# Operand transposes moved from TensorE to SP's DMA queue, and masking joined with the row maxima, in a three-stage graph kernel

## The chip, the cores and the metric

The kernel runs on one core of one Trainium2 chip. The metric is the device time of one execution in microseconds (us); the figure quoted is the median of three runs.

## What is computed

128 graphs of 128 nodes with 256 features each pass through one transformer layer (8 heads of 32, an additive bias and a mask from the adjacency matrix, an MLP of width 1024) and then through two single-head graph layers. Cut to what matters:

```python
nx = ln(x, ln1_g, ln1_b);  q, k, v = nx @ wq + bq, nx @ wk + bk, nx @ wv + bv     # 8 heads of 32
bias = where(adj > 0, 0.1 * adj * adj, -inf)
x1 = x + softmax(q @ k.T / sqrt(32) + bias) @ v @ wo + bo
x2 = x1 + gelu(ln(x1, ln2_g, ln2_b) @ w1 + b1) @ w2 + b2
for l in 0, 1:                                   # x starts as x2
    s = where(adj == 0, -1e10, (x @ Wq[l].T + bq[l]) @ (x @ Wk[l].T + bk[l]).T / sqrt(128))
    x = layer_norm(x + where(adj == 0, 0, softmax(s)) @ x @ Wc[l].T)
```

## The kernel before, in words

The graphs are worked in 32 groups of four (`B = 4`), so that one group has 512 rows of 256 features. Weights stay in SBUF. Float32 products are made of three float16 ones (`mm3`, lines 241 to 245): each operand is split into a high half (a cast) and a low half (what the cast lost).

A product needs its operand with the features on the partitions, while normalisations and residuals have the rows there. So five times for each group a block of 128 x 1024 values is turned: `N.xT` (normalised x, for q, k and v), `A.oT` (attention output, for `wo`), `M.mT` (normalised x1, for the MLP), `C0.xT` and `C1.xT` (the operands of the two graph layers). In each, TensorE makes 8 transposes of 128x128 float32 into PSUM (helper `transposes`, line 812, against the identity `ident`), ScalarE casts the result from PSUM into the high half (`xT_h`, `rot_h` or `cT_h`; lines 467, 493, 496, 513), and VectorE subtracts that from PSUM into the low half (`xT_l`, `rot_l`, `cT_l`; lines 654, 695, 710, 725).

For the softmax of the transformer layer, VectorE does two instructions for each graph over its 8 heads: `A.S` (line 673) scales the scores in PSUM, adds `biasA` and writes `area` in SBUF; `A.max` (line 678) reduces to the negated row maxima `nmax`. ScalarE then takes the exponential head by head (line 483). In a graph layer the same is `C.S` (line 731) and `C.max` (line 734), once for the four graphs.

There is no automatic scheduler. Five lists (`TENSOR`, `SCALAR`, `VECTOR`, `GPSIMD`, `SYNC`) give for each engine the order of its steps within one period. An entry such as `M.up3-2` is step `up3` of stage `M`, done for the group that lies two behind; one pass through a list is one period and the passes go over the 32 groups, so that about five groups are in work at once. Each step waits on semaphores for its inputs, and for the last reader of what it overwrites; on an engine everything is strictly in list order. `freed` (before each step of TensorE) holds the waits on PSUM banks.

SP's queue carries all steady DMA traffic: 12 small copies a group that stack q and k on 96 partitions for the scores (`Q.stk`, `qkS`), the load of x, two loads of the adjacency (`adj_in`), and the store of the result.

The steps that the prediction speaks of, on TensorE: `A.AV3` to `A.wo` (attention output of the last graph to the output projection), and `A.wo` to `M.up0` (the projection to the first MLP product). Between the latter lie `x1` (line 701), its statistics (lines 567 and 572), an inverse root on GpSimd (lines 396 and 398), the normalisation (line 580), and the turn `M.mT`.

Of the kernel before, what the change touches and what calls it, by code (L numbers as in the profile page):

```python
# [1073 lines left out]
```

## Time and profile before

| | |
|---|---|
| median of three runs | 2197.3 us (2193.87 to 2198.27) |
| the profiled execution | 2195.11 us, span 2193.1 us |
| busy: TensorE / VectorE / ScalarE / GpSimd | 2016.2 / 1721.4 / 1558.7 / 961.0 us |
| mean granted TensorE clock | 0.971 of full speed |
| DMA | 108.62 MB, mean 50 GB/s |

A busy time is the time in which an engine had at least one instruction in work; matmuls overlap one another, so their count times their mean length is more than it. A row of a group of instructions gives its busy time, the mean length of one in nanoseconds, and the idle time of the engine just before them. Idle time of an engine that is not the bottleneck costs nothing.

### The profile page before, as it was taken

Reading aid. Unit: us, or ns where it says so; the run is one execution under the profiler, and the core shown is the slowest. Engines: PE = TensorE matmul, PEld = TensorE weight load, DVE = VectorE, ACT = ScalarE, POOL = GpSimd, SP = SyncE. Lnnn points to the kernel's source line nnn. Section 1 sums busy time; section 2 is a strip of 40 time slices with the busy share of each in tenths; the row PEclk is TensorE's granted clock in tenths of the full one; section 3 lists DMA queues with packets and bytes.
Section 4 is the critical chain, followed back from the end, with each engine's and each line's share of the span. In section 5 each row is a group of like instructions: output and inputs, shape, how many; then the busy total and the mean of one; then the engine's idle time right before and its main releaser. Section 6 shows DMA issues by size and latency. Waiting matters only on the chain.

```text
span 2193.1 us, 45905 instructions
## 1 busy us (share of the span) xinstructions
PE 2016.2 (92%) x16984; PEld 1499.2 (68%) x16984; DVE 1721.4 (78%) x3397; ACT 1558.7 (71%) x2994; POOL 961.0 (44%) x1304
## 2 busy tenths in 40 slices
PE   5589899999999999999999999999999999999853
PEld 4356677777777777777777777777777777777531
DVE  4566788888888888888888888888888888887422
ACT  2367777777788777777787777777877777777521
POOL 2022344445454454444554544445545444544434
PEclk8799999999999999999999999999999999999976
DMA  3211012222211122222111222222111222210000
GB/s 106 73 49 42 28 45 58 59 59 56 58 49 42 33 59 59 59 59 54 49 42 35 57 58 59 59 54 57 43 39 44 59 59 59 54 50 16 15 10 19
DMA packets 103675, 108.62 MB, mean 50 GB/s; under 512 B 9824, under 2 KB 78432, under 8 KB 103456
## 3 DMA queue, kind: packets, MB, share of 16 engines
q1 hardware_dynamic: 102912, 104.90, 17.9%
q8 instruction: 138, 2.26, 0.4%
q0 software_dynamic: 544, 0.80, 0.2%
q14 instruction: 81, 0.66, 0.1%
HBM read 38.55 MB, written 16.78 MB: 25 GB/s over the span
## 4 chain that ended last, share of the span: by engine, by line
PE 72%; ACT 13%; DVE 6%; POOL 4%; issue 3%; DMA 2%; SPq 1%; DVEq 0%; POOLq 0%; ACTq 0%
PE ps L243 18%; PE ps L245 17%; PE ps L244 17%; PE ps L812 5%; PE ps L972 5%; PE ps L1046 5%; ACT area L483 4%; PE ps L1026 3%; POOL x L403 3%; ACT cs L525 2%; DMA out<-x 2%; ACT area L533 2%; ACT L525 2%; PE ps L965 1%; ACT cq L518 1%
## 5 line engine op out<-in xcount | busy, mean ns | idle before, releaser
L483 ACT ACTIVATE area<-area,nmax 128x128 f32<-128x128 f32 x1024 | 312.5, 390 | 0.8
L243 PE MATMUL ps<-w_h,hid_h 128*128 128x256 f16 x1024 | 279.1, 273 | 6.0 <-POOL hid_l L250 5.1
L245 PE MATMUL ps<-w_h,hid_l 128*128 128x256 f16 x1024 | 279.0, 272 | 0.0
L244 PE MATMUL ps<-w_l,hid_h 128*128 128x256 f16 x1024 | 279.0, 272 | 0.0
L396 POOL TENSOR_TENSOR ve<-mv,eps_cols 128x4 f32<-128x4 f32 x128 | 25.7, 201 | 572.0 <-DVE mv L572 572.0
L250 POOL TENSOR_TENSOR hid_l<-area,hid_h 128x512 f16<-128x512 f32 x128 | 151.8, 1186 | 251.9 <-ACT hid_h L506 251.9
L503 ACT ACTIVATE area<-ps,b_col 128x512 f32<-128x512 f32 x256 | 176.3, 689 | 77.9 <-PE ps L245 76.8
L403 POOL TENSOR_TENSOR x<-xh,cg_row 128x256 f32<-128x256 f32 x128 | 89.0, 728 | 295.7 <-DMA out<-x 272.6
L243 PE MATMUL ps<-rot_h,w_h 128*128 128x512 f16 x512 | 194.4, 380 | 6.2 <-ACT area L503 2.9
L245 PE MATMUL ps<-rot_h,w_l 128*128 128x512 f16 x512 | 194.0, 379 | 0.0
L244 PE MATMUL ps<-rot_l,w_h 128*128 128x512 f16 x512 | 193.9, 379 | 0.0
L518 ACT ACTIVATE ck<-ps,cb_col 128x512 f32<-128x512 f32 x64 | 44.1, 689 | 199.0 <-PE ps L245 199.0
L673 DVE SCALAR_TENSOR_TENSOR area<-ps,biasA 128x1024 f32<-128x1024 f32 x128 | 155.0, 1211 | 37.9 <-PE ps L965 37.9
L403 POOL TENSOR_TENSOR x<-x,cb_row 128x256 f32<-128x256 f32 x256 | 178.2, 728 | 5.0
L506 ACT CAST hid_h<-area 128x512 f16<-128x512 f32 x256 | 158.3, 618 | 8.1
L681 DVE SCALAR_TENSOR_TENSOR pT<-ps,pT 128x1024 f16<-128x1024 f32 x128 | 155.7, 1216 | 3.2 <-ACT pT L489 3.2
L812 PE MATMUL ps<-ident,area 128*128 128x128 f32 x1024 | 135.6, 276 | 21.6 <-DVE area L580 19.0
L678 DVE TENSOR_REDUCE nmax<-area 128x8 f32<-128x1024 f32 x128 | 154.8, 1210 | 0.2
L972 PE MATMUL ps<-ident,area 128*128 128x128 f32 x1024 | 136.3, 276 | 16.4 <-ACT area L483 11.3
L972 PEld LDWEIGHTS ps<-ident,area 128*128 128x128 f32 x1024 | 113.0, 141 | 45.2 <-DVE area L673 22.8
L243 PE MATMUL ps<-cw_h,cT_h 128*128 128x256 f16 x512 | 139.6, 273 | 3.9 <-DVE cs L731 3.9
L245 PE MATMUL ps<-cw_h,cT_l 128*128 128x256 f16 x512 | 139.6, 273 | 0.0
(178 smaller groups left out, 6214.0 us busy)
## 6 DMA issues: line engine op xcount, KB each, us to landing
qkS<-qk SPq DMA_DIRECT2D x384, 128.0 KB, 2.4
xin<-in_x SPq DMA_DIRECT2D x32, 512.0 KB, 3.8
adj_in<-in_adj SPq DMA_DIRECT2D x64, 256.0 KB, 2.9
out<-x SPq DMA_DIRECT2D x32, 512.0 KB, 3.9
area<-in_L_gnn_w SPq DMA_DIRECT2D x2, 1024.0 KB, 11.3
area<-in_L_gnn_Wc SPq DMA_DIRECT2D x2, 256.0 KB, 11.3
area<-in_L_gnn_wq SPq DMA_DIRECT2D x1, 256.0 KB, 3.7
area<-in_L_gnn_wk SPq DMA_DIRECT2D x1, 256.0 KB, 4.0
```

What stands on the lines that cost most here:

```text
L243: pe.matmul(dst, lh, rh, start=start, stop=False, **kw)
L244: pe.matmul(dst, lh, rl, start=False, stop=False, **kw)
L245: return pe.matmul(dst, ll, rh, start=False, stop=stop, **kw)
L403: last = pool.tensor_tensor(dst[:, b], src[:, b], row, op)
L483: last = act.activation(sc[:, b % 2, h], sc[:, b % 2, h], ACT.Exp, bias=nmax[:, b, h:h + 1])
L503: act.activation(hidden[:, b % 2, :], psUp, ACT.Gelu, bias=b1_col[:, b:b + 1], scale=1.0 / W_SCALE).then_inc(a_gelu, 1)
L506: act.copy(hid_h[:, b % RING, :], hidden[:, b % 2, :]).then_inc(a_hi, 1)
L673: dve.scalar_tensor_tensor(sc[:, b % 2], psA_heads, 1.0 / QK_SCALE, biasA[:, b].unsqueeze(1).broadcast_to([P, H, P]), ALU.mult, ALU.add).t ...
L678: dve.tensor_reduce(nmax[:, b, :], sc[:, b % 2], AX.X, ALU.max, negate=True).then_inc(d_max, 1)
L681: dve.scalar_tensor_tensor(pT16[:, b % 2, 1], psA_heads, P_SCALE, pT16[:, b % 2, 0], ALU.mult, ALU.subtract).then_inc(d_PT, 1)
L812: last = pe.transpose(dst[:, c, b * P:(b + 1) * P], rows[:, b, c * P:(c + 1) * P], ident[:, :])
L972: last = pe.transpose(psA_heads[:, h], sc[:, b % 2, h], ident[:, :])
```

## The change

It does two things, and gives all five lists new orders.

1. The transposes on TensorE go. ScalarE now casts the float32 rows themselves, before turning, into a float16 staging tile in SBUF (`sN_h`, `sA_h`, `sC_h`); VectorE subtracts into a second one (`sN_l`, `sA_l`, `sC_l`). SP then issues one DMA transpose for each half, 128x1024 float16 (8 blocks of 128x128), from the staging tile into `xT`, `rot` or `cT`. That is ten DMA transposes for each group. Consumers wait for both (`m_xT`, `m_oT`, `m_mT`, `m_cT`, of `TURN` = 32 for a pair).
2. `A.S` and `A.max` become one `tensor_tensor_reduce` per head, 8 for each graph, and `C.S` and `C.max` one per graph, 4 for each layer. They write negated scores (unscaled sum times -1/QK_SCALE) and their minimum; the exponential has `scale=-1.0`. `biasA`'s factor takes in `QK_SCALE`.

```diff
-SYNC = ["Q.stk-2", "N.ld-1", "Q.ldA-1", "M.ldC-3", "C1.sto-6"]
+SYNC = ["Q.stk-1", "N.ld+0", "M.mT-2", "C0.xT-3", "N.xT+0", "M.ldC-3", "Q.ldA+0", "C1.sto-5",
+        "C1.xT-4", "A.oT-1"]
...
+            def turn(g, dst_h, dst_l, src_h, src_l, a_made, d_made, m_done):
+
+                need_apart(sp, a_made, g, 1, 1)
+                sp.dma_start_transpose(dst_h.rearrange("p c (b t) -> p (c b) t", t=P),
+                                       src_h.rearrange("p c b d -> p (c b d)")).then_inc(m_done, 16)
+                need_apart(sp, d_made, g, 1, 1)
+                sp.dma_start_transpose(dst_l.rearrange("p c (b t) -> p (c b) t", t=P),
+                                       src_l.rearrange("p c b d -> p (c b d)")).then_inc(m_done, 16)
...
+                    elif what == "mT":
+
+                        need_apart(sp, t_wo, g, 1, 1)
+                        turn(g, rot_h, rot_l, sA_h, sA_l, a_mT, d_mT, m_mT)
...
-                        need(act, t_mT, g, 1, 1)
-                        act.copy(rot_h[:, :, :], psM).then_inc(a_mT, 1)
+                        need(act, d_xh[1], g, 1, 1)
+                        need(act, m_oT, g, TURN, TURN)
+                        act.copy(sA_h[:, :, :, :], by_chunk(xhat)).then_inc(a_mT, 1)
...
-                                                  bias=nmax[:, b, h:h + 1])
+                                                  bias=nmax[:, b, h:h + 1], scale=-1.0)
...
-                        dve.tensor_tensor(rot_l[:, :, :], psM, rot_h[:, :, :], ALU.subtract)\
+                        need(dve, m_oT, g, TURN, TURN)
+                        dve.tensor_tensor(sA_l[:, :, :, :], by_chunk(xhat), sA_h[:, :, :, :], ALU.subtract)\
...
-                        dve.scalar_tensor_tensor(sc[:, b % 2], psA_heads, 1.0 / QK_SCALE,
-                                                 biasA[:, b].unsqueeze(1).broadcast_to([P, H, P]),
-                                                 ALU.mult, ALU.add).then_inc(d_S, 1)
-                    elif stage == "A" and what[:3] == "max":
-                        need(dve, d_S, g, B, b + 1)
-                        dve.tensor_reduce(nmax[:, b, :], sc[:, b % 2], AX.X, ALU.max, negate=True).then_inc(d_max, 1)
+                        for h in range(H):
+                            last = dve.tensor_tensor_reduce(sc[:, b % 2, h], psA_heads[:, h], biasA[:, b],
+                                                            scale=-1.0 / QK_SCALE, scalar=HIGHEST,
+                                                            op0=ALU.add, op1=ALU.min,
+                                                            accum_out=nmax[:, b, h:h + 1])
+                        last.then_inc(d_S, 1)
...
-                            dve.tensor_tensor(cs[:, l], psC_S, biasC[:, g[1]], ALU.add).then_inc(d_cS[l], 1)
-                        elif what == "max":
-                            need(dve, d_cS[l], g, 1, 1)
-                            dve.tensor_reduce(cmax[:, l], cs[:, l], AX.X, ALU.max, negate=True).then_inc(d_cmax[l], 1)
+                            for b in range(B):
+                                last = dve.tensor_tensor_reduce(cs[:, l, b], psC_S[:, b], biasC[:, g[1], b],
+                                                                scale=-1.0, scalar=HIGHEST, op0=ALU.add,
+                                                                op1=ALU.min, accum_out=cmax[:, l, b:b + 1])
+                            last.then_inc(d_cS[l], 1)
...
-                        need(pe, d_mT, g, 1, 1)
+                        need(pe, m_mT, g, TURN, TURN)
```

What the lists made of this shows in the instructions as they stand. First **SP's queue**, one period before (the loads, the store and the twelve copies):

```order
L340 DMA qkS<-qk 32x2x1024 [waits t_S,a_qk0,d_qk0,a_qk1,d_qk1,a_qk2,d_qk2,a_qk3,d_qk3]
L340 DMA qkS<-qk 32x2x1024 x11
L330 DMA xin<-in_x 128x4x256 [waits d_x1]
L346 DMA adj_in<-in_adj 128x4x128 [waits d_mC,d_mA]
L351 DMA adj_in<-in_adj 128x4x128 [waits d_mA,d_mC]
L355 DMA out<-x 128x4x256 [waits p_c1]
```

and the part of a period of the changed kernel from `A.oT` to `N.xT` (of the stage `M.mT`, the tile is `rot` again):

```order
L338 DMA_TRANSPOSE rot_h<-sA_h 128x8x128 [waits t_up,a_oT]
L341 DMA_TRANSPOSE rot_l<-sA_l 128x8x128 [waits d_oT]
L377 DMA qkS<-qk 32x2x1024 [waits t_S,a_qk0,d_qk0,a_qk1,d_qk1,a_qk2,d_qk2,a_qk3,d_qk3]
L377 DMA qkS<-qk 32x2x1024 x11
L367 DMA xin<-in_x 128x4x256 [waits d_x1]
L338 DMA_TRANSPOSE rot_h<-sA_h 128x8x128 [waits t_wo,a_mT]
L341 DMA_TRANSPOSE rot_l<-sA_l 128x8x128 [waits d_mT]
L338 DMA_TRANSPOSE cT_h<-sC_h 128x8x128 [waits t_cW1,a_cT0]
L341 DMA_TRANSPOSE cT_l<-sC_l 128x8x128 [waits d_cT0]
L338 DMA_TRANSPOSE xT_h<-sN_h 128x8x128 [waits t_qk0,t_qk1,t_qk2,t_qk3,t_v0,t_v1,a_xT]
L341 DMA_TRANSPOSE xT_l<-sN_l 128x8x128 [waits d_xT]
```

The queue had six entries a period and has sixteen: `Q.stk` now stands right behind the pair of `A.oT`, and the pair of `M.mT` behind it and the load of x.

Second **TensorE** from `A.wo` (the first row) to `M.up0` (the last), the first instruction of each step; before:

```order
L243 MATMUL ps<-wo_h,rot_h 128x256 [waits d_oT]
...
L243 MATMUL ps<-cT_h,cqk_h 128x512 [waits d_cT1,d_cy0]
...
L965 MATMUL ps<-qkS 128x128 [waits stk,d_x1]
...
L1026 MATMUL ps<-ck,cq 128x128 [waits a_ck1,a_cq1]
...
L243 MATMUL ps<-wv_h,xT_h 128x256 [waits d_xT,a_gelu]
...
L243 MATMUL ps<-cw_h,cT_h 128x256 [waits d_cT1,a_ck1,d_cS1]
...
L812 MATMUL ps<-ident,area 128x128 [waits d_xh1,d_x2]
...
L243 MATMUL ps<-wv_h,xT_h 128x256 [waits d_xT,d_o]
...
L965 MATMUL ps<-qkS 128x128 [waits stk,d_S]
...
L1037 MATMUL ps<-ident,cs 128x128 [waits a_cexp1,a_cW1]
...
L243 MATMUL ps<-rot_h,w_h 128x512 [waits d_mT,d_v1]
```

and now:

```order
L250 MATMUL ps<-wo_h,rot_h 128x256 [waits m_oT,d_PT]
...
L250 MATMUL ps<-cT_h,cqk_h 128x512 [waits m_cT1,d_cy0]
...
L250 MATMUL ps<-wv_h,xT_h 128x256 [waits m_xT,a_gelu]
...
L250 MATMUL ps<-wv_h,xT_h 128x256 [waits m_xT,d_o]
...
L1039 MATMUL ps<-ck,cq 128x128 [waits a_ck1,a_cq1]
...
L990 MATMUL ps<-qkS 128x128 [waits stk,d_x1]
...
L250 MATMUL ps<-cw_h,cT_h 128x256 [waits m_cT1,a_ck1,d_cS1]
...
L990 MATMUL ps<-qkS 128x128 [waits stk,d_S]
...
L1050 MATMUL ps<-ident,cs 128x128 [waits a_cexp1,a_cW1]
...
L250 MATMUL ps<-rot_h,w_h 128x512 [waits m_mT,d_v1]
```

The same products stand between the two, without the eight transposes of `M.mT`; the last row now waits for the pair of DMA transposes (`m_mT`), not for VectorE.

Third **VectorE** from `A.xh` to `M.mT`, before:

```order
L567 BN_STATS st<-area 128x6 x3
L572 BN_AGGR mv<-st 128x2 [waits d_st1]
L572 BN_AGGR mv<-st 128x2 x3
L673 SCALAR_TENSOR_TENSOR area<-ps,biasA 128x1024 [waits t_PT,d_mA,t_S]
L731 TENSOR_TENSOR cs<-ps,biasC 128x512 [waits t_cPV1,d_mC,t_cS1]
L734 TENSOR_REDUCE cmax<-cs 128x4 [waits d_cS1]
L580 TENSOR_SCALAR area<-area,mv,rs 128x256 [waits p_rs1,d_mv1]
```

and now:

```order
L612 BN_AGGR mv<-st 128x2 x3
L775 TENSOR_TENSOR sC_l<-area,sC_h 128x1024 [waits m_cT1,a_cT0]
L620 TENSOR_SCALAR area<-area,mv,rs 128x256 [waits p_rs1,d_mv1,d_oT]
L620 TENSOR_SCALAR area<-area,mv,rs 128x256 x3
L782 ISA cs,cmax<-ps,biasC 128x128 [waits t_cPV1,d_mC,t_cS1]
L782 ISA cmax 128x1
...
L756 TENSOR_TENSOR sA_l<-area,sA_h 128x1024 [waits m_oT,a_mT]
```

A `tensor_tensor_reduce` is a pair of instructions here, the second with only the 128x1 result; and `C1.S` now stands between the normalisation and the subtraction of `M.mT` (last row), and waits for a product of TensorE (`t_cS1`).

## Rows read from the trace of the kernel before

**Rows 1.** Busy times over nine periods: us, PE, PEld, DVE, ACT, POOL, PEclk, DMA share, GB/s

```profile
347.29:909.15 561.86, 550.39 (x4754) 412.96 (x4753) 482.29 (x946) 435.06 (x838) 267.72 (x360) 1.00 0.20 52
```

**Rows 2.** Waits of TensorE from 347 to 1906 us: the longest in total

```profile
PE ps L1026 <- ACT cq L518: 9.4, 25, 0.4
```

**Rows 3.** Groups of TensorE by line and shape: the operand transposes

```profile
L812 PE MATMUL ps<-ident,area 128*128 128x128 f32 x1024 | 135.6, 276 | 21.6 <-DVE area L580 19.0 <-DVE x L751 1.8 <-DVE area L689 0.9
...
L812 PE MATMUL ps<-ident,xh 128*128 128x128 f32 x256 | 35.2, 282 | 16.5 <-DVE xh L580 15.2 <-ACT cs L537 1.4
```

**Rows 4.** Timeline of TensorE in one period: start us, length us, instruction, starts of steps

```profile
1098.81 1.13 PE L1026 MATMUL ps<-ck,cq 128*128 128x128 f32 x8 [0.38 <-ACT cq L518]
1099.77 0.27 PE L243 MATMUL ps<-wv_h,xT_h 128*128 128x256 f16 x1
...
1101.08 0.27 PE L243 MATMUL ps<-cw_h,cT_h 128*128 128x256 f16 x1
...
1103.70 1.04 PE L812 MATMUL ps<-ident,area 128*128 128x128 f32 x8
...
1110.09 1.97 PE L1046 MATMUL ps<-area,cs 128*128 128x256 f32 x8
...
1111.89 0.38 PE L243 MATMUL ps<-rot_h,w_h 128*128 128x512 f16 x1
...
1113.18 0.27 PE L243 MATMUL ps<-w_h,hid_h 128*128 128x256 f16 x1
...
1116.66 0.61 PE L965 MATMUL ps<-qkS 96*128 96x128 f16 x8
```

**Rows 5.** Timeline of VectorE in the same period

```profile
1095.43 1.23 DVE L701 SCALAR_TENSOR_TENSOR area<-ps,xin 128x1024 f32<-128x1024 f32 x1 [1.12 <-PE ps L245]
1096.69 1.41 DVE L567 BATCH_NORM_STATS2 st<-area 128x6 f32<-128x256 f32 x4
1098.24 0.38 DVE L572 BATCH_NORM_AGGREGATE mv<-st 128x2 f32<-128x6 f32 x4
...
1101.30 1.37 DVE L580 TENSOR_SCALAR area<-area,mv,rs 128x256 f32<-128x256 f32 x4
```

**Rows 6.** Timeline of GpSimd in the same period: the inverse root

```profile
1098.98 1.02 POOL L398 TENSOR_TENSOR rs<-ve,minus_half 128x4 f32<-128x4 f32 x1
```

**Rows 7.** Groups of VectorE by line and shape

```profile
L673 DVE SCALAR_TENSOR_TENSOR area<-ps,biasA 128x1024 f32<-128x1024 f32 x128 | 155.0, 1211 | 37.9 <-PE ps L965 37.9
L678 DVE TENSOR_REDUCE nmax<-area 128x8 f32<-128x1024 f32 x128 | 154.8, 1210 | 0.2
...
L689 DVE TENSOR_TENSOR area<-ps,rec 128x256 f32<-128x256 f32 x128 | 54.3, 424 | 4.4
...
L731 DVE TENSOR_TENSOR cs<-ps,biasC 128x512 f32<-128x512 f32 x64 | 44.3, 692 | 63.5 <-PE ps L1026 63.5
...
L734 DVE TENSOR_REDUCE cmax<-cs 128x4 f32<-128x512 f32 x64 | 43.6, 681 | 1.2
...
L710 DVE TENSOR_TENSOR rot_l<-ps,rot_h 128x1024 f16<-128x1024 f32 x32 | 38.9, 1215 | 4.2 <-ACT rot_h L496 4.2
...
L740 DVE SCALAR_TENSOR_TENSOR cscale<-cmax,crec 128x4 f32<-128x4 f32 x64 | 10.8, 169 | 2.2
...
L562 DVE SCALAR_TENSOR_TENSOR cqk_l<-ps,cgk,cqk_h 128x128 f16<-128x128 f32 x2 | 0.7, 341 | 0.0
```

**Rows 8.** Groups of ScalarE by line and shape: a cast of 1024 columns

```profile
L496 ACT CAST rot_h<-ps 128x1024 f16<-128x1024 f32 x32 | 32.4, 1012 | 12.6 <-PE ps L812 12.6
```

**Rows 9.** DMA issues: count, KB each, median us from issue to landing

```profile
qkS<-qk SPq DMA_DIRECT2D x384, 128.0 KB, 2.4
...
adj_in<-in_adj SPq DMA_DIRECT2D x64, 256.0 KB, 2.9
```

**Rows 10.** Timeline of SP's queue: the twelve copies

```profile
1021.63 7.82 SPq L340 DMA_DIRECT2D qkS<-qk  x12
```

**Rows 11.** DMA queue of SP: packets, MB, share of 16 engines' span

```profile
q1 hardware_dynamic: 102912, 104.90, 17.9%
```

More of the change, by code:

```diff
@@ L44 @@
 MASKED = -1e30
+HIGHEST = 3e38
 P_SCALE = 1024.0
@@ L251, in split_hidden, with by_chunk @@
                               hid_h[:, c % RING, :], ALU.subtract).then_inc(done, 1)
+        def by_chunk(rows):
+            return rows.rearrange("p b (c d) -> p c b d", c=KC)
         def steps(order, it, odd):
@@ L323, in weights @@
                 sp.dma_start(raw_w2, w2.rearrange("(c p) n -> p c n", p=P)).then_inc(ld_raw[2], 16)
+            def turn(g, dst_h, dst_l, src_h, src_l, a_made, d_made, m_done):
[5 more added lines that the diff above has]
+                                       src_l.rearrange("p c b d -> p (c b d)")).then_inc(m_done, 16)
             def iteration(it, odd):
                 for stage, what, g in steps(SYNC, it, odd):
-                    if stage == "N":
+                    if what == "xT" and stage == "N":
+                        for used in (*t_qk, *t_v):
+                            need_apart(sp, used, g, 1, 0)
+                        turn(g, xT_h, xT_l, sN_h, sN_l, a_xT, d_xT, m_xT)
+                    elif what == "oT":
+                        need_apart(sp, t_up, g, FC, 0)
+                        turn(g, rot_h, rot_l, sA_h, sA_l, a_oT, d_oT, m_oT)
+                    elif what == "mT":
+                        need_apart(sp, t_wo, g, 1, 1)
+                        turn(g, rot_h, rot_l, sA_h, sA_l, a_mT, d_mT, m_mT)
+                    elif what == "xT":
+                        l = int(stage[1])
+                        need_apart(sp, t_cW[1 - l], g, 1, -1 if l == 0 else 2)
+                        turn(g, cT_h, cT_l, sC_h, sC_l, a_cT[l], d_cT[l], m_cT[l])
+                    elif stage == "N":
                         need_apart(sp, d_x1, g, 1, -1)
@@ L463, in iteration @@
                     if stage == "N":
-                        need(act, t_xT, g, 1, 1)
-                        for used in (*t_qk, *t_v):
-                            need(act, used, g, 1, 0)
-                        act.copy(xT_h[:, :, :], psC).then_inc(a_xT, 1)
+                        need(act, d_xh[0], g, 1, 1)
+                        need(act, m_xT, g, TURN, 0)
+                        act.copy(sN_h[:, :, :, :], by_chunk(xhatN)).then_inc(a_xT, 1)
                     elif what in QK:
@@ L509, in iteration @@
                         if what == "xT":
-                            need(act, t_cT[l], g, 1, 1)
-                            need(act, t_cW[1 - l], g, 1, -1 if l == 0 else 2)
-                            act.copy(cT_h[:, :, :], psC).then_inc(a_cT[l], 1)
+                            if l == 0:
+                                need(act, d_x2, g, 1, 1)
+                                need(act, m_cT[1], g, TURN, -TURN)
+                            else:
+                                need(act, d_xh[2], g, 1, 1)
+                                need(act, m_cT[0], g, TURN, 2 * TURN)
+                            act.copy(sC_h[:, :, :, :], by_chunk((x2, xh3[:, :, :])[l])).then_inc(a_cT[l], 1)
                         elif what in ("q", "k"):
@@ L806, in _ @@
             pe.wait_ge(prep_dve, PREP_DVE)
-            def transposes(dst, rows, signal):
-                for c in range(KC):
-                    for b in range(B):
-                        last = pe.transpose(dst[:, c, b * P:(b + 1) * P], rows[:, b, c * P:(c + 1) * P],
-                                            ident[:, :])
-                last.then_inc(signal, 1)
             def to_columns(dst, w_h, w_l, x_h, x_l, n):
@@ L881, in iteration @@
                         freed(g, (d_S, 0, 4, 4))
+                    elif step == "A.AV1":
+                        freed(g, (d_o, 0, 4, 1))
+                    elif step == "Q.k1":
+                        freed(g, (d_qk[1], 0, 1, 1))
+                    elif step == "A.AV2":
+                        freed(g, (d_o, 0, 4, 2))
+                    elif step == "A.PT3":
+                        freed(g, (d_PT, 0, 4, 3))
                     elif step == "C0.xW":
```

189 lines of the change are left out of this document (85 added, 104 removed), and 25 rows, old and new, of tables (SCALAR, TENSOR, VECTOR).

## The prediction

> **What bounds the kernel now.** I read the busy times by stretch first, then TensorE's waits, then the timelines. Over nine periods of the steady part [rows 1] one period is 561.86/9 = 62.4 us; TensorE is busy 550.39/9 = 61.2 us of it at a granted clock of 1.00, VectorE 53.6, ScalarE 48.3, GpSimd 29.7. So TensorE bounds it, with 1.3 us a period unused, and its longest kind of wait is 9.4 us in 25 of them [rows 2]: the lists fit together almost without a gap. The 32 periods make 32 x 62.4 = 1997 us of the 2193; the rest, some 196 us, is filling and draining. What a period of TensorE loses, the run loses 32 times, if nothing else comes up to the bound.
>
> **What is taken from TensorE.** 1280 transposes go (1024 and 256), busy 135.6 + 35.2 = 170.8 us [rows 3], that is 40 a period at 133 ns, 5.3 us. TensorE's work falls to 61.2 - 5.3 = 55.9 us. With the same 1.3 us of gaps the period would be 57.2 us.
>
> **VectorE.** The subtractions of a turn stay (1215 ns for 1024 columns [rows 7]; the source is now SBUF and not PSUM, which I cost at nothing). Mask and maxima: before, a graph cost 1211 + 1210 ns and a graph layer 692 + 681 ns [rows 7]. Now a head costs one 128-column instruction and one that writes 128x1; call the pair d. The trace has no such pair. A column costs (1211 - 692)/512 = 1.0 ns, four 256-column instructions in a row take 1.37 us, 0.34 each [rows 5], so a 128-column one in a row takes 0.34 - 0.13 = 0.21 us; the smallest ones take 0.38/4 = 0.10 each in a row [rows 5]. That gives d = 0.31 us, the lower end. Without any overlap it is 341 + 169 ns [rows 7], d = 0.51, the upper end. I take 0.36, nearer the lower end, since the heads follow one another with no wait between. A period of VectorE is then 53.6 - 4 x 2.42 - 2 x 1.37 + 40d = 41.2 + 40d: 55.6 us at 0.36, 53.6 and 61.6 at the ends. So nothing is saved there; VectorE goes from 86% of a period to about 94%.
>
> Here a rule and the trace differ. The rows show that a 256-column instruction in a row costs as much (0.34) as a 128-column one costs alone (341 ns): neighbours overlap. The Trainium skill, VectorE: DVE Perf Modes, "The DRAIN you can't avoid", says that the next instruction starts only when the pipe is empty and that one should minimise the count of instructions. By that rule d is the upper end, a period of VectorE 61.6 us, and the time that of rival B at its end, 2225 us: it speaks against this half of the change; for plain instructions the rows speak against the rule.
>
> **ScalarE** does the same casts from SBUF (1012 ns [rows 8]) and 48.3 us a period; no bound.
>
> **What the DMA transposes cost.** No row shows one. Call X the time from the moment the low half stands in staging to both halves having landed. The nearest row by size is a load of 256 KB, 2.9 us from issue to landing; one of the stacking copies, 128 KB, takes 2.4 [rows 9], the lower end of X. For the upper end: a block's row is 128 float16, so a half is 1024 pieces of 256 bytes, 64 for each of 16 engines. The queue's 102912 packets took 17.9% of 2193 us on 16 engines [rows 11], 61 ns each. At 61 ns a piece a half takes 3.9 us; low waits behind high, which went 1.2 us earlier: 2 x 3.9 - 1.2 + 2.0 of latency (2.4 less a small transfer) = 8.6 us. By bytes the same queue moved 104.9 MB in 392 us, 267 GB/s, which makes 1.0 us of a half. I take X = 3.5 us, near the 2.9 of the row of the same size, a little over it for the smaller pieces. The Trainium skill gives 261 GB/s for a DMA transpose (DMA: Bandwidth & Descriptors, "Latency and other measured facts"), which would put a half at 1.0 us too.
>
> **Where X lies on the path.** In two places TensorE has too little work to hide it.
> *From A.wo to M.up0.* The chain after the projection's end: x1 1.23, statistics to the end of their aggregation 1.9 [rows 5], the inverse root (1.02 and a small one before it [rows 6]), beside which VectorE now does the subtraction of C0, 1.4 together, normalisation 1.37 [rows 5]: 5.9 us. Then comes C1.S on VectorE, which waits for TensorE's scores: products q and k at 1.29 (1111.89 to 1113.18 [rows 4]), two v at 1.31 (1099.77 to 1101.08), the scores 0.96: they end 6.2 us after the projection. With 4d = 1.4 and the subtraction 1.2 the low half stands at 8.8 us, and M.up0 can start at 8.8 + X. TensorE's work in between is 2 x 1.29 + 2 x 1.31 + 0.96 + xW 2.62 (1101.08 to 1103.70) + two A.S at 0.6 (1116.66) + four transposes 0.53 [rows 3, 4] = 10.5 us. X up to 1.7 us is hidden; beyond it the period is 55.9 - 10.5 + 8.8 + X = 54.2 + X, 57.7 us at X = 3.5. The stall is 1.8 us a period.
> *From A.AV3 to A.wo.* Work in between: up7 1.29, PT 0.53, PV 1.80 (1110.09 to 1111.89), three down at 1.31: 7.55 us. Chain: reciprocal and product 0.17 + 0.42 [rows 7] with a small gap, cast 1.01, subtraction 1.22: 2.95. X up to 4.6 us is hidden.
> Where both stall, the period is 55.9 - 10.5 - 7.55 + 8.8 + 2.95 + 2X = 49.6 + 2X.
>
> **SP's queue.** What is moved behind the transposes: the twelve copies follow directly on the pair of A.oT. They take 7.82 us to issue [rows 10] and some 1.8 more to land; A.S0, which waits for them, comes 2.6 (A.wo) + 6.2 us after that pair has landed. They come in time as long as the queue itself is held for less than about 2.7 us by one transpose. The loads and the store behind them are hidden by a period of slack, the queue being idle most of it. Ten transposes at 1 us beside 17.9% of 62 us in the engines leave them under half busy.
>
> **The sum.** Period 57.7 + 1.3 = 59.0 us; 32 x (62.4 - 59.0) = 109 us less. In filling and draining each of five turns costs X in place of 8 x 133 ns, 5 x 2.5 = 12 us more. Against the profiled execution's 2195.1 us: 2195 - 109 + 12 = 2098; the median of the three runs lies 2.2 us above that execution: 2100 us. This case's own range is 2055 to 2150 (X from 2.4 to 4.6, d from 0.31 to 0.41).
>
> **Rivals.**
> *A. All is hidden.* X under 1.7 us, or chains that give way: 57.2 a period, 2195 - 166 + 2 = 2031 us. For it: 1.0 us of data for a half. Against: neither DMA row lands under 2.4 us [rows 9].
> *B. VectorE becomes the bound.* From 41.2 + 40d > 57.7, d > 0.41. Halfway at 0.44 it is 58.8 + 1.3 = 60.1 us, 2195 - 74 + 14 = 2135; at 0.51, 62.9 us, 2225. The second instruction of a pair reads a result that the first has just finished, which may take the overlap away.
> *C. Slower: X from A.wo to M.up0 and from A.AV3 to A.wo.* Both stall, and the gain is gone at 49.6 + 2X + 1.3 > 62.4, X > 5.8 us. At the upper end, 8.6, the period is 68.1 and the time 2195 + 182 + 38 = 2415 us. For it: pieces of 256 bytes, and that high and low go one behind the other on one queue. Against: 267 GB/s on the same queue.
> *D. Block by block.* If SP issues the 8 blocks of a half one after another at the price of a stacking copy (7.82/12 = 0.65 us), a half holds the queue for 5.2 us, ten take 52, with the copies and loads 61: X = 2 x 5.2 - 1.2 + 1.8 = 11 us, period 73, time about 2580 us. The Trainium skill (VectorE: DVE Perf Modes, "The three transpose paths") gives 1309 ns for a 128x128 block by DMA against 390 on TensorE; eight in a row would be 10.5 us a half, over 110 us a period and some 3800 us, by an estimate from that page. No run here shows it, and a price for one block alone has the latency in it.
> That the change does nothing can be left out: the transposes are gone from TensorE's order.
>
> **Chances.** The forecast 0.55, A 0.08, B 0.12, C 0.17, D 0.08. A measurement of this kernel can tell about 0.2% (4 us) from no change. Faster by more: the forecast, A and nearly all of B but its upper end, 0.73; within 0.2%: the edges of B and C, 0.04; slower: the rest, 0.23. The range starts at A, 2030, and goes to 2320, which takes in the lower half of C and leaves out its upper half, D and a little below A: 0.18.
>
> **What would show it.** TensorE busy near 1846 us (2016 - 171), one wait a period of 1 to 2 us at the first product of `rot` for the DMA, none at `wo`. DMA transposes landing 2.5 to 4 us after issue. VectorE near 1790 us, its pairs 0.3 to 0.4 us start to start. The load of x every 59 us. I am wrong if the transposes land after more than 5 us, if TensorE waits at three or more of the five turns, or if VectorE is above 97% of a period.

## The result, and the profile after

The changed kernel takes 2293.7 us (median of 4 runs, 2293.0 to 2295.9) against 2195.7 us for the kernel before beside it: a ratio of 1.0444, 95% interval 1.0432 to 1.0457. It is 98 us slower; the forecast was 2100 us, faster. Its profiled execution has a span of 2294.0 us against 2193.1.

The page of the changed kernel, busy time of each engine and SP's queue:

```profile
PE 1901.0 (83%) x15704; PEld 1349.2 (59%) x15704; DVE 1641.6 (72%) x5573; ACT 1559.6 (68%) x2994; POOL 1049.4 (46%) x1304
...
q1 hardware_dynamic: 440832, 188.82, 34.9%
```

Busy time over twenty periods, from one x1 to another (the columns of [rows 1]), first of the changed kernel, then of the kernel before over the same stretch of work:

```profile
423.12:1748.07 1324.95, 1155.96 (x9761) 824.33 (x9760) 1015.89 (x3460) 967.40 (x1860) 654.93 (x800) 0.99 0.38 88
```

```profile
408.16:1655.19 1247.03, 1223.15 (x10562) 917.60 (x10561) 1069.87 (x2101) 966.79 (x1860) 595.16 (x800) 1.00 0.20 52
```

A period went from 62.35 to 66.25 us. The second is a mean of two stretches: from one x1 to the next it is 65.6 to 68.6 us until 1095 us and 65.2 to 65.6 from there on. TensorE is busy 57.8 us of it (61.2 before) and unused for 8.45 (1.2 before). VectorE went down, from 53.5 to 50.8 us, ScalarE stayed at 48.4: no engine is near full. 32 x 3.90 = 125 us more in the periods, less 24 in filling and draining (198 before, 174 after), make the 101 us between the spans.

The waits of TensorE from 400 to 1850 us, 21.9 periods: us in total, times, longest. Before, the longest kind was 9.4 us in 25 periods [rows 2].

```profile
PE ps L250 <- POOL hid_l L257: 47.3, 22, 3.5
PE ps L250 <- DVE cmax L782: 30.4, 22, 1.7
PE ps L250 <- ACT area L540: 22.9, 22, 1.3
PE ps L997 <- DVE nmax L716: 22.3, 22, 1.0
PE ps L990 <- DVE nmax L716: 21.7, 22, 1.0
PE ps L1059 <- POOL area L440: 19.8, 22, 1.0
PE ps L990 <- DVE pT L723: 19.5, 22, 0.9
PE ps L250 <- DMA rot_l<-sA_l: 0.6, 3, 0.2
```

Seven kinds, each once a period, on three engines; the last line is the transposes' landing, 0.6 us in 21.9 periods. The transposes themselves, from the DMA issues (count, median us from issue to landing) and from the timeline of SP's queue:

```profile
rot_h<-sA_h SPq DMA_TRANSPOSE x64, 2.8
rot_l<-sA_l SPq DMA_TRANSPOSE x64, 2.8
cT_h<-sC_h SPq DMA_TRANSPOSE x64, 2.7
```

```profile
1075.84 0.37 SPq L383 DMA_DIRECT2D adj_in<-in_adj  x1
1076.33 0.44 SPq L392 DMA_DIRECT2D out<-x  x1
...
1083.19 1.23 SPq L338 DMA_TRANSPOSE rot_h<-sA_h  x1
1084.60 1.23 SPq L341 DMA_TRANSPOSE rot_l<-sA_l  x1
1086.52 7.98 SPq L377 DMA_DIRECT2D qkS<-qk  x12
```

The one-instruction pairs, groups of VectorE:

```profile
L716 DVE CUSTOM_DVE_ANT_0 area<-ps,biasA 128x128 f32<-128x128 f32 x1024 | 225.0, 284 | 20.4 <-PE ps L990 17.1
L716 DVE DVE_READ_ACCUMULATOR2_ANT nmax<- 128x1 f32 x1024 | 84.1, 82 | 0.0
```

So the parts are cheap. The loss is in how they are lined up. Its largest piece in one period follows (timelines of GpSimd, VectorE and TensorE; the number in brackets is idle time before). The steps in it: `M.lo7` makes the low half of the last eighth of the MLP's hidden values, for TensorE's `M.down7`; `C0.af` is the scale and shift at the end of the first graph layer, `C0.PV` that layer's attention output; `M.mC` makes the mask of the graph layers; `Q.ldA` loads the adjacency; `C1.sto` stores the result.

```profile
1081.32 3.77 POOL L440 TENSOR_TENSOR x<-xh,cg_row 128x256 f32<-128x256 f32 x4 [12.04 <-DMA out<-x]
1085.16 2.77 POOL L440 TENSOR_TENSOR x<-x,cb_row 128x256 f32<-128x256 f32 x4
1087.89 1.16 POOL L257 TENSOR_TENSOR hid_l<-area,hid_h 128x512 f16<-128x512 f32 x1
```

```profile
1075.26 0.42 DVE L684 TENSOR_SCALAR biasC<-adj_in 128x512 bf16<-128x512 int32 x1
...
1088.13 1.66 DVE L803 SCALAR_TENSOR_TENSOR xh<-ps,cscale,area 128x256 f32<-128x256 f32 x4 [3.02 <-POOL x L440]
...
1094.91 1.22 DVE L745 SCALAR_TENSOR_TENSOR area<-ps,xin 128x1024 f32<-128x1024 f32 x1 [2.20 <-PE ps L252]
```

```profile
1089.10 0.28 PE L250 MATMUL ps<-w_h,hid_h 128*128 128x256 f16 x1 [2.12 <-POOL hid_l L257]
```

VectorE's M.mC frees `adj_in` at 1075.7; behind that, in SP's list, stands the load Q.ldA, and behind the load the store C1.sto, issued at 1076.33. GpSimd's C0.af overwrites the stored x, so it waits until the store has landed and starts at 1081.32. C0.af holds M.lo7 behind it until 1087.89; TensorE waits 2.1 us for that half at down7, wo comes late, and x1 with it.

### The profile page after: what moved, and what is told of

It reads as the page before. It is cut to its first block and busy times, and to the rows that moved or that the text cites. A ratio compares the mean times of both kernels' runs of the same rounds, so it can differ in the third digit from the quotient of the medians.

```text
span 2294.0 us, 46475 instructions
## 1 busy us (share of the span) xinstructions
PE 1901.0 (83%) x15704; PEld 1349.2 (59%) x15704; DVE 1641.6 (72%) x5573; ACT 1559.6 (68%) x2994; POOL 1049.4 (46%) x1304
## 3 DMA queue, kind: packets, MB, share of 16 engines
q1 hardware_dynamic: 440832, 188.82, 34.9%
## 5 line engine op out<-in xcount | busy, mean ns | idle before, releaser
L433 POOL TENSOR_TENSOR ve<-mv,eps_cols 128x4 f32<-128x4 f32 x128 | 77.5, 605 | 490.6 <-DVE mv L612 490.6
L440 POOL TENSOR_TENSOR x<-xh,cg_row 128x256 f32<-128x256 f32 x128 | 126.2, 1017 | 321.7 <-DMA out<-x 320.5
L716 DVE CUSTOM_DVE_ANT_0 area<-ps,biasA 128x128 f32<-128x128 f32 x1024 | 225.0, 284 | 20.4 <-PE ps L990 17.1
L558 ACT ACTIVATE cq<-ps,cb_col 128x512 f32<-128x512 f32 x64 | 43.8, 685 | 280.9 <-PE ps L252 280.9
L440 POOL TENSOR_TENSOR x<-x,cb_row 128x256 f32<-128x256 f32 x256 | 193.4, 787 | 5.0
L440 POOL TENSOR_TENSOR area<-area,cwb_row 128x256 f32<-128x256 f32 x128 | 89.0, 726 | 224.7 <-ACT area L573 224.7
L701 DVE SCALAR_TENSOR_TENSOR qk<-ps,bqk_col,qk 128x512 f16<-128x512 f32 x128 | 95.4, 745 | 132.5 <-ACT qk L508 132.5
L525 ACT ACTIVATE pT<-ps 128x1024 f16<-128x1024 f32 x128 | 130.7, 1021 | 53.5 <-PE ps L997 51.7
L997 PE MATMUL ps<-ident,area 128*128 128x128 f32 x1024 | 138.9, 280 | 33.9 <-DVE nmax L716 30.4
L1059 PE MATMUL ps<-area,cs 128*128 128x256 f32 x512 | 129.0, 397 | 34.1 <-POOL area L440 33.3
```

The lines of the kernel that those rows point to most:

```text
L440: last = pool.tensor_tensor(dst[:, b], src[:, b], row, op)
L525: act.activation(pT16[:, b % 2, 0], psA_heads, ACT.Copy, scale=P_SCALE).then_inc(a_PT, 1)
L716: last = dve.tensor_tensor_reduce(sc[:, b % 2, h], psA_heads[:, h], biasA[:, b], scale=-1.0 / QK_SCALE, scalar=HIGHEST, op0=ALU.add, op1=A ...
L997: last = pe.transpose(psA_heads[:, h], sc[:, b % 2, h], ident[:, :])
```

## The experiments

Each kernel was timed in 3 rounds (5 for the last two) beside the kernel before. Period, TensorE's busy time and unused time per period (all in us) are worked out for each as above, over twenty periods. The letters of the theories are those of the expectations; T is the landing of the transposes in e1 to e8, and from e9 on that is called X, while T there is TensorE's own order with its PSUM banks.

| kernel | time, us | ratio to before (95%) | period | busy | unused |
|---|---|---|---|---|---|
| before | 2195 to 2198 | 1 | 62.35 | 61.16 | 1.19 |
| the change | 2293.7 | 1.044 (1.043 to 1.046) | 66.25 | 57.80 | 8.45 |
| e1 | 2240.7 | 1.020 (1.018 to 1.022) | 64.02 | 57.46 | 6.56 |
| e2 | 2201.2 | 1.002 (1.001 to 1.003) | 62.50 | 61.22 | 1.28 |
| e3 | 2350.5 | 1.070 (1.068 to 1.073) | 67.79 | 58.01 | 9.77 |
| e4 | 2428.2 | 1.106 (1.104 to 1.108) | 70.30 | 59.83 | 10.48 |
| e5 | 2240.6 | 1.019 (1.016 to 1.021) | 64.00 | 57.23 | 6.77 |
| e6 | 2231.0 | 1.014 (1.012 to 1.017) | 63.78 | 57.26 | 6.52 |
| e7 | 2193.6 | 0.998 (0.997 to 1.000) | 62.75 | 61.21 | 1.53 |
| e8 | 2564.9 | 1.166 (1.164 to 1.169) | 74.57 | 61.28 | 13.29 |
| e9 | 2215.9 | 1.009 (1.006 to 1.011) | 62.97 | 57.35 | 5.62 |
| e10 | 2216.8 | 1.009 (1.007 to 1.011) | 63.10 | 57.24 | 5.86 |
| e11 | 2175.9 | 0.991 (0.989 to 0.992) | 61.69 | 57.10 | 4.59 |
| e12 | 2201.7 | 1.002 (1.001 to 1.003) | 62.39 | 57.67 | 4.72 |
| e13 | 2171.2 | 0.988 (0.986 to 0.991) | 61.23 | 57.62 | 3.61 |
| e14 | 2177.2 | 0.991 (0.989 to 0.994) | 61.40 | 57.72 | 3.68 |
| e15 | 2241.3 | 1.020 (1.018 to 1.022) | 63.86 | 57.89 | 5.97 |
| e16 | 2149.8 | 0.977 (0.976 to 0.979) | 60.56 | 57.23 | 3.33 |
| e17 | 2156.3 | 0.982 (0.980 to 0.984) | 61.07 | 57.18 | 3.89 |

### The parts, and the store

**e1: the store ahead of the load.**

```
- "M.ldC-3", "Q.ldA+0", "C1.sto-5",
+ "M.ldC-3", "C1.sto-5", "Q.ldA+0",
```

> The changed kernel with one entry of SP's list moved: the store of the result (C1.sto) stands ahead of the adjacency load Q.ldA and no longer behind it. Theory S (circle through the store): each period the store waits behind Q.ldA for VectorE's mask of C0, its landing (4 us) holds GpSimd's C0.af, and that holds C0.PV on VectorE (3.0 us idle) and the last low half on GpSimd (TensorE 2.1 us idle). It expects these two waits to go and the period to fall from 66 us by 3 to 4.5 us: 2150 to 2200 us. Theory T (the landing of the DMA transposes makes the period long): no change, 2285 to 2300 us.

53 us less than the change, 2.2 us a period; the wait for `hid_l` falls from 2.1 to 0.2 us, and VectorE no longer waits for GpSimd at C0.PV (3.3 us a period before). Of the other six kinds, that for `cmax` falls from 1.4 to 1.0 us and five stay as they were; TensorE now waits 0.4 us a period for the stacking copies. Theory S had the right mechanism and missed its range of 2150 to 2200; the store was half of the loss. Theory T, at 2285 us or more, is out.

```profile
PE ps L250 <- POOL hid_l L257: 5.2, 23, 0.2
PE ps L990 <- DMA qkS<-qk: 8.0, 11, 1.0
```

**e2: the pairs alone**, in the kernel before (the entries `max` leave its lists).

```
- dve.scalar_tensor_tensor(sc[:, b % 2], psA_heads, ...)
- dve.tensor_reduce(nmax[:, b, :], sc[:, b % 2], AX.X, ALU.max, negate=True)
+ for h in range(H):
+     last = dve.tensor_tensor_reduce(sc[:, b % 2, h], ..., accum_out=nmax[:, b, h:h + 1])
```

> The kernel before, with its own lists and TensorE's transposes, and only the mask and maxima in one instruction per head. By the 0.21 us a head seen after, VectorE loses some 3.5 us a period. Theory S and T alike: TensorE stays the bound (61.2 of 62.4 us), so 2185 to 2198 us. Theory P (the pairs do harm, by lengthening the way to the exponential or by holding GpSimd off the shared memory port): over 2205 us.

VectorE does 3.5 us a period less and nothing comes of it, 3 us above what was expected: TensorE is full (61.2 of 62.5 us).

**e3: the moved transposes alone**: the changed kernel with mask and maxima in two instructions (the reverse of e2's edit).

> The changed kernel with mask and maxima again as two instructions a graph (the second right behind the first), in the changed kernel's lists. VectorE gets 3.5 us a period more. Theory S: VectorE lies on the circle between C0.PV and the mask of C0, so nearly all of it is added, 2370 to 2410 us. Theory T: the turns have room for it on VectorE, 2290 to 2320 us. Theory P: under 2290 us.

57 us slower than the change, between the ranges of S and T, so neither had the size. VectorE has slack in both, and still its instructions cost time: the first sign that it lies on the path though it is not full.

**e4 and e5: GpSimd's order.** e4 is e1 with M.lo7 ahead of C0.af, e5 is e1 with M.lo3 ahead of C1.af.

```
e4  - "A.x1b-1", "C0.af-3", "M.lo7-1"]     + "A.x1b-1", "M.lo7-1", "C0.af-3"]
e5  - "C1.rs-4", "C1.af-4", "M.lo3-1",     + "C1.rs-4", "M.lo3-1", "C1.af-4",
```

> As the kernel with the store moved, and on GpSimd the last low half (M.lo7) ahead of C0.af. Theory S: with the store early, C0.af starts when C0's normalisation is done and TensorE's wait for the last low half is gone either way; against the first kernel 0 to 1 us a period less, 2120 to 2200 us; or, if C0.af behind lo7 then holds C0.PV, up to 3 us a period more than it. Theory T: 2285 to 2300 us.

> The kernel with the store early (2240.7 us), and on GpSimd the low half M.lo3 ahead of C1.af (the scale and shift of the second graph layer), as the lists before had it. Theory C (the period is a closed chain through the orders of VectorE, ScalarE and GpSimd): ScalarE's up5 waited 0.9 us for lo3 behind C1.af and VectorE's q0 3.9 us for ScalarE; that chain gets up to 0.9 us a period shorter, 2210 to 2235 us. Theory T (the landing of the DMA transposes is what makes the period long): 2235 to 2245 us.

e4 is 187 us slower than e1, above every range: the half now stands in front of C0.af, VectorE's C0.PV waits 8.6 us each time for C0.af, and TensorE for both. Of the 6.3 us that a period is longer than in e1, 2.4 are TensorE's work, at a granted clock of 0.96 in the mean of its periods.

```profile
DVE xh L803 <- POOL x L440: 180.8, 21, 9.0
```

e5 changes nothing: the range of T, not that of C.

**e6 and e7: no table loads on ScalarE's way to down7.** GELU is replaced by the identity, in e1 and in the kernel before, so both compute something else.

```
- psUp, ACT.Gelu,        + psUp, ACT.Identity,
```

> The kernel with the store early (2240.7 us), its eight GELUs a group replaced by the identity function, so that the computation is changed and ScalarE has no table loads (six a period at 1.28 us, 7.7 us). Theory C: table loads lie on the closed chain (that of up7 between A.oT and A.wo, that of up4 ahead of q0), so the period falls by 2.5 to 5 us, 2080 to 2160 us. Theory T: only the part of the chain that is not the transposes' falls, by under 1 us a period, over 2210 us.

> The kernel before with the same replacement of GELU by the identity. TensorE is 98% busy in its period and ScalarE has slack, so theory C expects next to nothing, 2180 to 2197 us. If it falls by more than 20 us, the kernel before was bound through ScalarE too.

10 and 4 us. Theory C had expected 80 us or more of the first, so that ScalarE's table loads set the period falls; T's range holds.

**e8: both parts of the change in the lists of before** (the turns' entries are taken out, the transposes go into SP's list where their halves come up).

> Both parts of the change in the lists of the kernel before: the steps xT, oT and mT taken out of TensorE's list and the maxima out of VectorE's, nothing else moved, and the five pairs of DMA transposes put into SP's list where their inputs come ready. Worked out from the timeline of before with 2.8 us from issue to landing: stalls of 1.6 us at A.wo, 2 at A.S0 (stacking copies behind the transposes), 3 at M.up0, 1 at C0.q: period 63 to 65 us, 2220 to 2280 us. Theory T: as long as the new lists or longer, 2280 to 2340 us, since the landings are not hidden here. Theory L (the new lists are what costs): clearly under the changed kernel's 2294, 2150 to 2260 us.

Slower still, and by 225 us or more above the ranges of all three theories. Its waits of TensorE from 400 to 1850 us:

```profile
PE ps L252 <- DMA rot_l<-sA_l: 87.9, 39, 3.6
PE ps L992 <- DMA qkS<-qk: 65.8, 19, 4.7
```

Here landing and queue are the largest waits, 4.5 and 3.4 us a period, and TensorE's work is 61.3 us, with a granted clock of 0.95 in the mean. The new lists had taken those waits away and paid for it in others. Only one place of the transposes in SP's list was tried, so that the old lists must be this slow with them is not shown.

### The chain that returns

No theory on record held for all of these: T's ranges fit e5 and e6, and e1 rules it out. I followed the releasers back from an instruction of e5 in the middle of its run, through several periods: the same sequence returns each time, with all of its 64 us, about half of it on VectorE, a quarter on TensorE and none on a DMA. From x1: A.st, GpSimd's inverse root, A.xh, ScalarE's cast, VectorE's steps in list order to C1.st, GpSimd's root again, C1.xh, A.PT0; then TensorE to q0, ScalarE's part of q0, and VectorE's C0.xh, the pairs of A.S3 and the last A.AV; ScalarE's cast of oT, M.up7; GpSimd's M.lo7; TensorE's down7 and wo; x1. The waits of e5 from 400 to 1850 us that lie on it, and the landing, which does not:

```profile
PE ps L990 <- DVE pT L723: 39.1, 22, 1.8
DVE qk L701 <- ACT qk L508: 91.0, 44, 3.6
PE ps L250 <- DMA rot_l<-sA_l: 1.5, 4, 0.8
```

The timeline of VectorE in e5 shows two places where a step stands in the wrong order on it:

```profile
1146.96 2.27 DVE L620 TENSOR_SCALAR x<-x,mv,rs 128x256 f32<-128x256 f32 x4 [1.25 <-POOL rs L435]
...
1149.76 1.21 DVE L723 SCALAR_TENSOR_TENSOR pT<-ps,pT 128x1024 f16<-128x1024 f32 x1
...
1161.08 0.75 DVE L701 SCALAR_TENSOR_TENSOR qk<-ps,bqk_col,qk 128x512 f16<-128x512 f32 x1 [3.63 <-ACT qk L508]
1161.75 1.74 DVE L620 TENSOR_SCALAR xh<-xh,mv,rs 128x256 f32<-128x256 f32 x4
```

A.PT0 (1149.76), for which TensorE waits, stands behind C1.xh, which waits; C0.xh (1161.75) stands behind a wait of 3.63 us although its input is old, and A.S3's pairs behind it. Nothing is added or removed in what follows.

```
e9, on e1   - "Q.q0+0", "C0.xh-4", "A.S3-1",    + "C0.xh-4", "Q.q0+0", "A.S3-1",
e10, on e5  - "C1.xh-5", "M.lo2-2", "A.PT0-1",  + "M.lo2-2", "A.PT0-1", "C1.xh-5",
e11         both of them, on e5
```

> e1_store_early with one swap in VectorE's list: C0's normalisation xh (the 1.7 to 2.4 us at L620 that stands between the step Q.q0 and the pairs of A.S3) goes ahead of Q.q0, where VectorE waits 3.6 us for ScalarE's part of q0. No work is added or taken away, and no engine was full. Theory V (the period is a closed chain of waits along VectorE's hand-written order: x1 after wo, A.xh, A.S0, A.S1, C1.PV, the waits for GpSimd's rs, A.PT0, then TensorE to q0, VectorE's xh and A.S3's pairs, the last A.AV, the oT cast, down7 and wo, back to x1): the chain gets 1.6 us shorter in each of 33 periods, 2240 less about 50: 2180 to 2205, ratio 0.99 to 1.003. Theory X (the transposes' landing or SP's queue sets the period) and theory T (TensorE's own order with its PSUM banks does): 2235 to 2245, no change against e1.

> e5 (which alone brought nothing over e1) with the steps M.lo2 and A.PT0 of VectorE ahead of C1.xh, so that they run while VectorE waits 1.25 us for GpSimd's rs, and no longer behind the 2.3 us of C1.xh. Theory V: A.PT0 starts up to 2.9 us earlier, TensorE's wait of 1.8 us for it goes, and the closed chain is 1.8 to 2.9 us shorter per period: 2150 to 2185. Theories X and T: 2235 to 2245.

> Both moves of e9 and e10 in one kernel (with e5's and e1's). Theory V: the gains add up as far as no other chain is next: 3.4 to 4.5 us per period, 2095 to 2135, faster than the kernel before (ratio 0.955 to 0.97), with TensorE's busy share at 88% or more; the next limit is TensorE's own 55.9 us. Theories X and T: 2235 to 2245; if only one of the two moves was on the chain, no better than the better of e9 and e10.

Each alone is worth 24 us, both 65 us (2.3 us a period), with every engine doing the same work. That shows that the order of VectorE's list sets the period though VectorE is not full; theories X and T, which had no change, fall. That the entries are links of one closed chain is read from the releasers, and the moves agree with it. The sizes were set too high (1.0 and 0.9 us a period for 1.6 and 1.8 to 2.9, and 2176 us for 2095 to 2135 in e11). That both together give more than the sum fits other chains close behind. In e11, besides, C0.xh runs beside GpSimd's N.xb and M.lo5 and takes twice as long:

```profile
1188.12 3.58 DVE L620 TENSOR_SCALAR xh<-xh,mv,rs 128x256 f32<-128x256 f32 x4
```

### What is left in it

```
e12, on e11  ScalarE  - "N.xT+0", "M.up2-2",           + "M.up2-2", "N.xT+0",
e13, on e12  VectorE  "Q.v1" from ahead of A.S0 to between A.st and A.xh
e14, on e13  VectorE  "M.mT" from ahead of A.S0 to behind it
e15, on e11  mask and maxima in two instructions, as in e3
e16, on e11  VectorE  Q.v1 as in e13, without e12's swap
```

> e11 (2175.9) with one swap in ScalarE's list: M.up2 ahead of N.xT. ScalarE waits 1.5 us for VectorE's normalised x there, with the eviction of up2 queued behind it, and TensorE then waits 1.0 us for up2's PSUM buffer. Theory V (chain of waits along the hand-written lists): that wait lies on the chain that returns every period, so 0.6 to 1.0 us less per period: 2142 to 2158. If the chain passes elsewhere (rival: TensorE's wait there is slack that comes back at A.S2): 2172 to 2178.

Missed, with the wrong sign: 26 us slower than e11. ScalarE in e12:

```profile
1189.96 0.69 ACT L540 ACTIVATE area<-ps,b_col 128x512 f32<-128x512 f32 x1 [2.42 <-DVE hid_l L257]
1190.68 0.62 ACT L543 CAST hid_h<-area 128x512 f16<-128x512 f32 x1
1191.20 1.04 ACT L503 CAST sN_h<-area 128x1024 f16<-128x1024 f32 x1
```

and VectorE:

```profile
1192.27 1.23 DVE L696 TENSOR_TENSOR sN_l<-area,sN_h 128x1024 f16<-128x1024 f32 x1 [0.59 <-ACT sN_h L503]
...
1194.02 1.22 DVE L723 SCALAR_TENSOR_TENSOR pT<-ps,pT 128x1024 f16<-128x1024 f32 x1
```

up2 needs a buffer that VectorE's M.lo0 has still to read, so it waits 2.4 us for VectorE; the cast of N.xT now stands behind that, VectorE's N.xT waits for the cast, and A.PT0 stands behind N.xT. I had looked at who waits for up2, and not at what up2 waits for.

> e12 with VectorE's step Q.v1 (v_l, 0.6 us) taken from in front of A.S0 and put into the 1.3 us in which VectorE waits for GpSimd's rs between A.st and A.xh. Theory V: another 0.4 to 0.6 us per period, 13 to 20 us less than e12. Rival (the wait for rs hides nothing, or v's PSUM comes too late for it): e12 within 3 us.

> e13 with VectorE's M.mT (sA_l, 1.2 us) behind A.S0 and no longer ahead of it. Theory V: A.S0's maxima are out 1.2 to 1.5 us earlier, TensorE's wait of 1.0 us for them before A.S1 goes; but sA_l and its transposes come 1.7 us later, and M.up0 now waits for their landing 1.5 to 2 us, so that the gain is given back in part: between 20 us faster and 20 us slower than e13. Theory X (landing time of the transposes binds): slower than e13 by 30 us or more.

> e11 with mask and maxima in two instructions again, as in the kernel before (e3's edit). In the order of the change that cost 57 us. If VectorE's instructions of A.S0, A.S1, A.S3 and C1.S lie on the closed chain still, the price stays: 2225 to 2245, slower than the kernel before. If e11's chain has moved to TensorE for the most part: 2185 to 2205. So this tells what the pairs alone are worth beside the moved transposes.

> e11 with e13's move alone (VectorE's Q.v1 in the wait for GpSimd's rs), ScalarE's list as in the change. Theory V, as mended by e12 (the chain that returns runs from x1 through VectorE's list to N.xh and from there through ScalarE's N.xT or VectorE's N.xT, whichever is later): e12's loss and e13's gain add up independently, so e11 less 15 to 30 us: 2146 to 2161, ratio 0.977 to 0.984. If e13's gain only made good what e12 had lost, 2170 to 2177.

e13 is 30 us under e12 (13 to 20 expected), and e16 26 us under e11: the 0.6 us of v_l fit into VectorE's wait for the root. e14 gains nothing (+6 us), as expected of it; theory X had asked for 30 us or more. e15 is 65 us over e11 and slower than the kernel before: with TensorE at 93% of a period in e11 the pairs are still worth 2.2 us a period, and without them the moved transposes don't pay even in e11's order. e16 beats both kernels, at 0.9773 (0.9755 to 0.9791). The lists of the kernel before were not mended in the same way; they had 1.2 us of unused time a period to give. Its twenty periods, and its two longest kinds of waits of TensorE from 400 to 1850 us:

```profile
412.61:1623.71 1211.10, 1144.60 (x9761) 819.84 (x9760) 1026.32 (x3460) 963.00 (x1860) 648.31 (x800) 1.00 0.41 97
```

```profile
PE ps L250 <- DVE cmax L782: 26.2, 24, 1.4
PE ps L1059 <- POOL area L440: 23.0, 24, 1.2
```

Followed back like e5, the chain of e16 is TensorE's own work for about half of its time, and VectorE's for about an eighth.

### A neighbour that isn't free

**e17: the subtraction away from the inverse root.** In the changed kernel VectorE, then GpSimd:

```profile
1098.02 1.19 DVE L775 TENSOR_TENSOR sC_l<-area,sC_h 128x1024 f16<-128x1024 f32 x1
1100.51 0.73 DVE L620 TENSOR_SCALAR area<-area,mv,rs 128x256 f32<-128x256 f32 x2 [1.30 <-POOL rs L435]
```

```profile
1098.18 1.09 POOL L433 TENSOR_TENSOR ve<-mv,eps_cols 128x4 f32<-128x4 f32 x1 [9.13 <-DVE mv L612]
1099.35 1.02 POOL L435 TENSOR_TENSOR rs<-ve,minus_half 128x4 f32<-128x4 f32 x1
```

The first instruction of the root, of 4 columns, takes 1.09 us. Its group in the kernel before, where the subtractions read PSUM:

```profile
L396 POOL TENSOR_TENSOR ve<-mv,eps_cols 128x4 f32<-128x4 f32 x128 | 25.7, 201 | 572.0 <-DVE mv L572 572.0
```

```
- "A.st-1", "C0.xT-2", "Q.v1+0", "A.xh-1", "C1.S-4", "M.mT-1"]
+ "A.st-1", "Q.v1+0", "A.xh-1", "C1.S-4", "C0.xT-2", "M.mT-1"]
```

> e16 with VectorE's C0.xT (sC_l, 1.2 us, two SBUF operands) taken from between A.st and A.xh, where GpSimd computes the inverse root beside it, and put behind C1.S. Theory P (such a subtraction on VectorE holds up a GpSimd instruction that starts beside it until it ends): the first small GpSimd instruction of that root takes 0.20 us there and no longer 1.09, its mean over the kernel falls from 604 to about 400 ns, and A.xh starts 0.6 to 0.9 us earlier after x1. The 1.2 us of sC_l are no longer covered, so A.S0 comes 0 to 0.6 us later: the time stays within 15 us of e16, 2135 to 2165. Rival (the 1.09 us belong to the instruction, after an idle stretch of GpSimd): its mean stays at 600, A.xh starts no earlier.

The same group in e17, and one of its instructions from the timeline:

```profile
L433 POOL TENSOR_TENSOR ve<-mv,eps_cols 128x4 f32<-128x4 f32 x128 | 50.0, 390 | 488.4 <-DVE mv L612 488.4
```

```profile
1083.41 0.20 POOL L433 TENSOR_TENSOR ve<-mv,eps_cols 128x4 f32<-128x4 f32 x1 [7.46 <-DVE mv L612]
```

The mean falls from 604 to 390 ns, and at this place it is 0.20 us after an idle stretch as long. In e16, 58 of the 128 take 1.09 us, and all of them start beside a VectorE subtraction with two SBUF operands (`sC_l` 31, `sN_l` 27); in e17 only the 27 are left. So theory P holds: such a subtraction holds GpSimd up. A.xh starts 1.5 us after the statistics' end and no longer 2.4. With the 1.2 us uncovered the kernel is 6 us slower than e16 (10 by the ratios), within what was expected: the 0.9 us won at the root don't show in the time.

## Why the prediction was wrong

**The step that failed** is "With the same 1.3 us of gaps the period would be 57.2 us", and with it "In two places TensorE has too little work to hide it". The gaps of before were a property of its lists. New lists are a new fit, of which I looked at the two stretches where the transposes lie, and took the rest to be as tight as before. Measured, the period is 66.25 us for 59.0: 1.9 us from TensorE's work (57.8 for 55.9), 5.35 from unused time (8.45 for 1.3 + 1.8). At the two places named (M.up0 and wo) the landing takes 0.6 us in 22 periods. The stated signs of being wrong did not warn either: the landings took 2.8 us in the median and not over 5, TensorE waited for them from 400 to 1850 us at no third turn, and VectorE was busy for 77% of a period and not over 97%. All three look at the parts and none at the gaps.

**What took its place**: a closed chain from x1 to x1 through VectorE's list and those of GpSimd, ScalarE and TensorE, and through SP's store. What e1, e9, e10, e11, e13 and e16 show is that the lists made the loss: 5.7 us of a period (66.25 to 60.56) came back by moving five entries. The links between them are read from the traces. Rival C gave the sign, by a mechanism that is not there: it needs X over 5.8 us. None of the rivals had this one, a wait on an engine that is not full, outside the transposes.

**TensorE's 5.3 us** was too much. I took the mean of a group whose instructions overlap their neighbours' ends; a turn of eight starts at 1103.70 [rows 4] and what follows it 0.88 us later, 0.11 us each, 4.4 us a period. That leaves 56.8, and e16 has 57.2. In the changed kernel the granted clock falls now and then as well (below).

**VectorE**: d = 0.36 us was too high and even its lower end, 0.31, was: pairs start every 0.21 us, as the 128-column price from the rows alone would have it, with nothing for the second instruction. I had set the Trainium skill against it (VectorE: DVE Perf Modes, "The DRAIN you can't avoid") and left out that this section itself lets an instruction that is not held start earlier. When one is held is told in the section behind it, "Two Vector instructions with no wait between them": it counts an op with an accumulator as two instructions and holds neither where their operands start in the same quadrant; the trace agrees, the 82 ns of the second lie inside the next first one. VectorE's load was therefore forecast too high (55.6, measured 50.8), and rival B falls.

**X** was near: 2.8 us from issue to landing with the low half issued 0.1 us after it stands, some 2.9 against 3.5 taken and inside its bounds of 2.4 and 8.6. Rival D falls: eight blocks hold the queue for 1.23 us.

**"The source is now SBUF and not PSUM, which I cost at nothing"**: e17 shows a price, 0.9 us of GpSimd where such a subtraction stands beside a root. It is no new work on VectorE, so I did not see it.

**SP's queue**: "The loads and the store behind them are hidden by a period of slack". The store was not: it stood behind a load that waits for VectorE, and that cost 2.2 us a period (e1). I had costed time in the queue, not the order in it. The twelve copies were in time, as forecast.

**What stays open**: why the first half of the changed kernel's run has the longer periods; of the last 3.3 us of gaps in e16 the waits for the maxima of C1.S (1.1 us) and for GpSimd's C1.cWb, the bias that it adds to the second graph layer's product (1.0 us), are the largest, and neither was tried.

## What to carry to other kernels

Where every engine follows a hand-made list, the gaps belong to the lists: a change that comes with new ones is costed by following one whole chain from a step back to itself a period later, through every list, and the moved work is only one term of it. Of each entry that is moved ask both questions: who is queued behind it, and what does it wait for itself. No engine need be full for that chain to set the period: that idle time of an engine that is not the bottleneck costs nothing holds only where nobody waits for what stands behind it. Moves of five entries, which add and remove no work, were worth 5.7 us a period here, more than the 4.4 us of work that the change took away.
